# The last batch of a Mamba and mixture-of-experts layer: scans in two halves of 256 tokens, and experts without sorting

## The reference, cut to what matters

```python
x, z = split(in_proj(h))                      # 1024 inner channels each
x = silu(causal_conv4(x) + conv_b)
dt_lo, B, C = split(x_proj(x))                # 32, 16, 16
delta = softplus(dt_proj(dt_lo) + dt_b)
state[n] = exp(delta * A[n]) * state[n] + delta * x * B[n]   # over 512 tokens, for 16 states n
y = sum_n(C[n] * state[n]) + D * x
h = layernorm(h + out_proj(y * silu(z)))
logits = h @ gate.T                           # 8 experts, the best 2, softmax over the 2
h = layernorm(h + sum_over_2(w * (expert[e] @ h + expert_b[e])))
```

## Time and profile before

| what | value |
| --- | --- |
| median of 3 executions | 2401.52 us (2400.4 to 2407.32) |
| the profiled execution's own time | 2402.95 us |
| its span, first to last instruction | 2401.1 us |
| mean granted TensorE clock | 0.907 of full |
| busy: TensorE, VectorE, ScalarE, GpSimd | 87%, 87%, 63%, 76% |
| last scan ends at | 2221.6 us |

### The profile page before, as it was taken

One profiled execution on the slowest core, in us unless ns is written; L12 is line 12 of the kernel. 1 busy time (PEld: TensorE's weight loads), 2 busy tenths in 40 slices (PEclk: granted clock), 3 DMA queues, 4 the chain that ended last, 5 costly groups with the idle time before them and its releaser, 6 DMA issues.

```text
span 2401.1 us, 29781 instructions
## 1 busy us (share of the span) xinstructions
PE 2088.5 (87%) x8544; PEld 1217.3 (51%) x8544; DVE 2080.6 (87%) x2284; ACT 1516.3 (63%) x2586; POOL 1817.9 (76%) x1460
## 2 busy tenths in 40 slices
PE   7886879898989989899889989899898989888874
PEld 2444555555545555545545555545555555554532
DVE  3799999999999899998999989989999889999400
ACT  3747755785577766677577765768566775545322
POOL 1859997788887888779887888869887788776212
PEclk9897789898998999999899999989998899779887
DMA  3412031357544574356743674436752475477394
GB/s 99 145 53 84 19 125 60 114 176 256 155 111 145 198 263 123 106 165 216 269 110 116 210 265 130 128 137 207 257 133 91 156 244 180 127 233 235 76 378 120
DMA packets 210752, 385.08 MB, mean 160 GB/s; under 512 B 29048, under 2 KB 29304, under 8 KB 210592
## 3 DMA queue, kind: packets, MB, share of 16 engines
q1 hardware_dynamic: 196256, 349.63, 43.5%
q0 software_dynamic: 14336, 33.56, 6.7%
HBM read 297.15 MB, written 85.98 MB: 160 GB/s over the span
## 4 chain that ended last, share of the span: by engine, by line
DVE 27%; PE 22%; POOL 18%; issue 11%; ACT 4%; DMA 3%; SPq 1%; DVEq 0%; POOLq 0%; ACTq 0%
DVE hst L1432 14%; PE bank L873 13%; POOL dbu L1268 11%; DVE y L1290 7%; PE hTp L885 5%; DVE u L1318 2%; POOL u L1256 2%; POOL delta L1253 2%; PE bank L991 1%; DMA zs<-sorted_tokens 1%; ACT tokT L1143 1%; ACT dA L1180 1%; PE hTp L919 1%; DVE st L1296 1%; POOL sorted_tokens L1204 1%
## 5 line engine op out<-in xcount | busy, mean ns | idle before, releaser
L1268 POOL TENSOR_TENSOR dbu<-u,Bbc 128x512 f32<-128x512 f32 x1024 | 1308.1, 1313 | 298.0 <-DVE hst L1432 293.1
L1432 DVE TENSOR_TENSOR_SCAN hst<-dA,dbu 128x512 f32<-128x512 f32 x1024 | 1200.4, 1205 | 29.1 <-ACT dA L1180 25.9
L1180 ACT ACTIVATE dA<-delta,negA 128x512 f32<-128x512 f32 x1024 | 701.9, 689 | 477.8 <-DVE hst L1432 475.9
L885 PE MATMUL hTp<-ident,hst 128*128 128x128 f32 x4096 | 592.1, 298 | 124.5 <-DVE y L1290 43.9
L885 PEld LDWEIGHTS hTp<-ident,hst 128*128 128x128 f32 x4096 | 515.8, 154 | 363.9 <-DVE y L1290 143.9
L1290 DVE SCALAR_TENSOR_TENSOR y<-hTp,Ct,y 128x1024 f32<-128x1024 f32 x512 | 646.0, 1262 | 41.8 <-PE hTp L885 38.4
L873 PE MATMUL bank<-wslot,hidT 128*128 128x512 f32 x512 | 241.7, 607 | 16.7 <-ACT zs L1132 13.0
L873 PE MATMUL bank<-delta,tokT 128*128 128x512 f32 x536 | 248.3, 600 | 4.1 <-issue 2.2
L873 PE MATMUL bank<-wslot,tokT 128*128 128x512 f32 x496 | 236.5, 607 | 6.6 <-ACT tokT L1143 4.7
L873 PE MATMUL bank<-hidT,wslot 128*128 128x512 f32 x384 | 190.2, 639 | 12.8 <-DVE u L1318 9.7
L1318 DVE SCALAR_TENSOR_TENSOR u<-bank,cw,u 128x511 f32<-128x511 f32 (+2 forms) x192 | 142.3, 743 | 32.9 <-ACT u L1065 28.0
(11 more groups left out here) (131 smaller groups left out, 2238.8 us busy)
## 6 DMA issues: line engine op xcount, KB each, us to landing
wslot<-in_w_expT SPq DMA_DIRECT2D x86, 1024.0 KB
Bbc<-b_scratch SPq DMA_DIRECT2D x128, 256.0 KB
sorted_results<-ysb SPq DMA_DIRECT2D x113, 256.0 KB, 5.8
zs<-sorted_tokens SPq DMA_DIRECT2D x105, 256.0 KB, 4.0
wslot<-in_w_inT SPq DMA_DIRECT2D x26, 1024.0 KB
res<-in_w_expT SPq DMA_DIRECT2D x18, 1024.0 KB, 5.7
gate_scratch<-zs SPq DMA_DIRECT2D x64, 256.0 KB, 2.0
spare<-gate_scratch SPq DMA_DIRECT2D x56, 256.0 KB, 5.2
```

The lines of the kernel that those rows point to most:

```text
L885: mm = nc.tensor.transpose(hTp[i % 2][:, tok(j)], hst[n % 2][:, j, tok(i)], ident[:, :])
L1180: nc.scalar.activation(dA[j % 2][:, :], delta[w.odd][:, j, :], ACT.Exp, scale=negA[:, j, n:n + 1]).then_inc(exp_done, 1)
L1268: nc.gpsimd.tensor_tensor(dbu[j % 4][:, :], u[w.odd][:, j, :], Bbc[n % 2][:, :], ALU.mult).then_inc(dbu_done, 1)
L1432: nc.vector.tensor_tensor_scan(hst[n % 2][:, j, :], dA[j % 2][:, :], dbu[j % 4][:, :], 0.0, ALU.mult, ALU.add).then_inc(scan_done, 1)
```

## The change

Four things change.

1. `SEG_EPI` scans batch 7 in two halves of 256 tokens, all 16 states of the first half and then all of the second: 256 steps of half the length. ScalarE's and VectorE's instructions become 256 of 256 tokens; GpSimd's stay 128, each for two channel tiles; the transposition groups and additions stay 64 of 128 tokens, two a state and half, one for every four steps. The last column of each first-half scan is kept in `hst` and is the start of the second-half scan. B is loaded in 32 half rows.
2. Under the second half stand the first half's multiplication by z, output projection, normalization and gating, and its first six experts (`gyF` to `denF`). The experts are not sorted: each of the two tiles is multiplied by each expert (four matrix products) and VectorE adds the product with the token's weight, zero for experts not chosen, to `res` (`den`, `denF`). Experts 0 to 5 are loaded one after the other (`load_F`); 3 to 7 stay for the tail.
3. `SEG_LAST` has the same for tiles 2 and 3: `yT`, `out`, `ln1`, `x1T`, `logits`, gating for two tiles, then 20 dense products (experts 6 and 7 for tiles 0 and 1, all 8 for tiles 2 and 3), bias, normalization and store. Count, place, scale, scatter, the sorted tiles of batch 7 and `SEG_END` are gone. Experts 0 to 2 are loaded again (`load_D`). The gate values of batch 6 are loaded in four loads of 512 KB to places of their own (`szE`) in place of eight of 256 KB through two buffers. The bonuses of `SEG_EPI` and its pace are others.
4. In the segments from batch 3 on, ScalarE's eviction of the previous segment's last sorted tile (the eleventh) stands after the exponential of the second step, not before that of the first. This holds at five boundaries.

The planner's orders of `SEG_TWO` and `SEG_FULL` are otherwise the same. The diff, cut to its core:

```diff
+FIRST_EXPERTS = 6
+KEPT_SLOTS = [15, 16, 0, 1, 14, 15, 16, 0]
+GONE = range(NE - 5)
+KEPT = range(NE - 5, NE)
+LAST_DEN = [(t, e) for t in range(PAIR) for e in range(FIRST_EXPERTS, NE)] + [(t, e) for t in range(PAIR, NT) for e in [*KEPT, *GONE]]
...
+        "load_F": [("sp", 0.5, [(("gy", 4 * k + 3), "pool", 0.1)] if k < 2 else [(("moe", TILES - 5 + k), "pe", 0.1)] if k < 5 else [(("denF", 2 * (k - 5) + 1), "pe", 0.1)])],
+        "gyF": [("pool", 1.4, [(("row", 132 + 4 * (k // HALF)), "dve", 0.1), (("next_z", NT - 1), "sp", 4)])],
+        "yTF": [("pe", turn, [(("gyF", k), "pool", 0.1), (("outF", k // HALF - 1), "pe", 0), (("moeL", TILES - 1), "pe", 0)]), ("act", 0.6, [(x, "pe", 0.1)])],
+        "outF": [("pe", mm, [(("yTF", 2 * k + 1), "act", 0.1)]), ("dve", 1.8, [(x, "pe", 0.1), (("next_res", k), "sp", 6)])],
+        "lnF": [("act", 1.7, [(("outF", k), "dve", 0.1)])],
+        "x1TF": [("pe", turn, [(("lnF", k), "act", 0.1)]), ("act", 0.6, [(x, "pe", 0.1)])],
+        "logF": [("pe", 1.2, [(("x1TF", k), "act", 0.1)])],
+        "gateF": [("dve", 1.8, [(("logF", 1), "pe", 0.1)]), ("act", 0.3, [(x, "dve", 0.1)])],
+        "routeF": [("dve", 1.2, [(("gateF", 0), "act", 0.1)])],
+        "wTF": [("pe", 0.7, [(("routeF", 0), "dve", 0.1)]), ("act", 0.6, [(x, "pe", 0.1)])],
+        "denF": [("pe", mm, [(("x1TF", k % PAIR), "act", 0.1), (("logF", 1), "pe", 0), (("load_F", k // PAIR), "sp", 8)] if name == "denF" else []),
+                 ("dve", 0.75, [(x, "pe", 0.1), (("routeF", 0), "dve", 0)] + [(("denF", k - 2), "dve", 0)] * (k > 1))],
...
+def part_rows(halved):
+
+    return [2 * r for r in range(NH + 1)] + list(range(3 * NH, 2 * STEPS, NH)) if halved else list(range(0, STEPS, 2))
...
+SEG_EPI = Segment(by_urgency({"L0": 1114, "L1": 620, "mw": 161, "m0": 117, "ld": 51, "oe": -588, "of": 483, "ln": -83, "sc": 157, "mb": -398, "m1": -167, "E0": -758, "E1": 716, "m2": 204, "m3": 279, "m4": -375, "nz": -189, "ha": 293, "hd": 241, "lz": 54}), 0.45,
+                  W_EPI + W_O + GAP + [experts(2, TILES) + KEPT_IN[14], KEPT_IN[15], KEPT_IN[16]], [], 2 * STEPS)
+LAST_ROWS = [x for t in range(PAIR, NT) for x in [("yT", HALF * t + h) for h in range(HALF)] + [("out", t), ("ln1", t), ("x1T", t), ("logits", t)]]
+SEG_LAST = Segment([("load_D", e) for e in GONE] + LAST_ROWS + [("gate", 1), ("route", 1), ("wT", 1)]
+                   + [x for i in range(len(LAST_DEN)) for x in [("den", i)] + [("bias", t) for t in range(NT) if ("den", i) in last_den(t)]]
+                   + [x for t in range(NT) for x in (("fest", t), ("fln2", t), ("fstore", t))] + END, 0, W_LAST, [], 0)
...
+        def early_z(t, first, stop):
+
+            if t < PAIR:
+                return hT[:, HALF * t + first:HALF * t + stop, :]
+            return u[0][:, HALF * t + first:HALF * t + stop, :]
...
+        def part_of(q, halved):
+
+            per = PAIR if halved else NH
+            n, c, i = q // per % NS, q // per // NS, q % per
+            return n, PAIR * c + i, columns(n, c, halved)[0] + i * P
+
+        def columns(n, c, halved):
+
+            if not halved:
+                return 0, L
+            first = NS // 2 - n // 2 if c == 0 else 0
+            return first, first + HL
+
+        def decay_of(step, halved):
+
+            if halved:
+                return dA[step // 2 % 2][:, step % 2 * HL:(step % 2 + 1) * HL]
+            return dA[step % 2][:, :]
...
+                elif name == "load_F":
+                    e = x[1]
+                    if e < 2:
+                        sync.wait_ge(gy_done, w.e * (HALF * NT) + PAIR * HALF * (e + 1))
+                    else:
+                        s, v = w.bank(("moe", TILES - 5 + e) if e < 5 else ("denF", 2 * (e - 5) + 1))
+                        sync.wait_ge(bank_full[s], v)
+                    sync.sem_inc(seen_sp, 1)
+                    sync.dma_start(slot_of(w, KEPT_SLOTS[e]), block_src(("We", e))).then_inc(w_loaded[KEPT_SLOTS[e]], 16)
...
-                            sync.wait_ge(dbu_done, w.b * (NS * ND) + n * ND)
+                        if not (w.seg is SEG_PRO and m == 0):
+                            sync.wait_ge(dbu_done, w.b * (NS * ND) + m * (ND // 2 if w.seg.halved else ND))
                             sync.sem_inc(seen_sp, 1)
-                        if n + 1 < NS:
-                            load_B(w.b, n + 1)
...
-                    pe.wait_ge(acc_done, G * NH + (i - 1))
+            def state_part(b, q, halved, first, turns):
+
+                n, _, start = part_of(q, halved)
+                per = PAIR if halved else NH
+                if q % per == 0:
+                    pe.wait_ge(scan_done, b * (NS * ND) + (q // per + 1) * ND)
+                if not (first and q < 2):
+                    pe.wait_ge(acc_done, b * (NS * NH) + (q - 1))
                 if not (isinstance(turns, int) and turns == 0):
                     pe.wait_ge(turned_taken, turns)
                 for j in range(ND):
-                    mm = nc.tensor.transpose(hTp[i % 2][:, tok(j)], hst[n % 2][:, j, tok(i)], ident[:, :])
+                    mm = nc.tensor.transpose(hTp[q % 2][:, tok(j)], hst[n % 2][:, j, start:start + P], ident[:, :])
...
+                elif name in ("den", "denF"):
+                    t = LAST_DEN[x[1]][0] if name == "den" else x[1] % PAIR
+                    final = w if w.tail else w.final
+                    if share == 0:
+                        pe.wait_ge(turned_taken, (w.before.final if name == "den" and t < PAIR else final).turn(("x1T", t))[2])
+                    mm = accumulate(ps[:, :], lambda i: x1_turned(final, t)[:, tok(i)], lambda i: W[:, i, :], KD, share)
...
+            def decay(w, step):
+                n, j, halved = step // ND % NS, step % ND, w.seg.halved
+                cols = slice(step // STEPS * HL, (step // STEPS + 1) * HL) if halved else slice(0, L)
+                scans = max(step - 2, -1) if halved else step - 1
+                if step < ND:
                     act.wait_ge(u_ready, w.b * ND + (j + 1))
-                if not (w.seg is SEG_PRO and n == 0 and j < 2):
-                    act.wait_ge(scan_done, w.b * (NS * ND) + (n * ND + j - 1))
-                nc.scalar.activation(dA[j % 2][:, :], delta[w.odd][:, j, :], ACT.Exp, scale=negA[:, j, n:n + 1]).then_inc(exp_done, 1)
+                if not (w.seg is SEG_PRO and step < 2) and not (halved and step % 2):
+                    act.wait_ge(scan_done, w.b * (NS * ND) + scans)
+                nc.scalar.activation(decay_of(step, halved), delta[w.odd][:, j, cols], ACT.Exp, scale=negA[:, j, n:n + 1]).then_inc(exp_done, 1)
...
+                    if step == 1 and w.b > 2 and w.seg.steps:
+                        piece(w.before, ("moe", LATE - 1))
                     for x in pieces:
-                        piece(w, x)
-
-            periods(act, period, period, period)
+                        if w.seg is not SEG_FULL or x != ("moe", LATE - 1):
+                            piece(w, x)
+
...
+                    elif w.seg.halved and j % 2 == 0:
+                        k, cols = step // 2, slice(n // NS * HL, (n // NS + 1) * HL)
+                        if j == 0:
+                            pool.wait_ge(b_loaded[n % 2], w.b * (16 * NS // 2) + 16 * (n // 2 + 1))
+                        if n == 0:
+                            pool.wait_ge(u_ready, w.b * ND + (j + 2))
+                        pool.wait_ge(scan_done, w.b * (NS * ND) + (k - 3 if k < 4 else 2 * k - 6))
+                        nc.gpsimd.tensor_tensor(dbu[k % 4][:, :].rearrange("p (k t) -> p k t", k=2), u[w.odd][:, j:j + 2, cols],
+                                                Bbc[n % 2][:, cols].unsqueeze(1).broadcast_to((P, 2, HL)), ALU.mult).then_inc(dbu_done, 1)
...
+                elif name in ("den", "denF"):
+                    t, e = LAST_DEN[x[1]] if name == "den" else (x[1] % PAIR, x[1] // PAIR)
+                    dve.wait_ge(wt_ready, NB + t // PAIR)
+                    before = [i for i in range(x[1]) if LAST_DEN[i][0] == t] if name == "den" else []
+                    if before:
+                        sl, vl = w.bank(("den", before[-1]))
+                        dve.wait_ge(bank_taken[sl], vl)
+                    elif name == "den" and t < PAIR:
+                        sl, vl = w.before.bank(("denF", PAIR * (FIRST_EXPERTS - 1) + t))
+                        dve.wait_ge(bank_taken[sl], vl)
+                    elif name == "denF" and e > 0:
+                        sl, vl = w.bank(("denF", x[1] - PAIR))
+                        dve.wait_ge(bank_taken[sl], vl)
+                    nc.vector.scalar_tensor_tensor(res[:, t, :], ps[:, :], wt[:, t, e:e + 1], res[:, t, :], ALU.mult, ALU.add).then_inc(bank_taken[s], 1)
...
+                    elif w.seg.halved:
+                        c = n // NS
+                        start, stop = columns(n % NS, c, True)
+                        kept = columns(n % NS, 0, True)[1] - 1
```

(35 more changed lines are left out.)

466 lines of the change are left out of this document (280 added, 186 removed).

## The result

The changed kernel took a median of **2393.95 us** (20 executions, 2388.04 to 2401.65) beside 2407.02 for the kernel before in the same sessions (20 executions, 2394.7 to 2421.09). The ratio is 0.9952, with a 95% interval of 0.9938 to 0.9967: 13.1 us faster on the medians, where 2350 us, some 51 us faster, was forecast, and outside the range of 2328 to 2382. So the spans differ by less than the medians do, and I compare stretches rather than spans.

What follows compares the result with a forecast made beforehand. VectorE was taken to set the last batch's pace, with TensorE having room, before a serial tail of 180 us. 2402.95 + 37 (scans) - 78.5 (tail) - 10 (boundaries) = 2351.5, against the median 2350 us; range 2328 to 2382.

Steps and rivals of the forecast that it cites:

- The last batch's scans: Last batch, 256 half-length scans with first-half work added: 37 us longer, to 287 us (range +22 to +60).
- the tap: Second-half scans starting from a memory column: 0.055 us more each, 7 us for 128, from a similar instruction (0.743 against 0.69).
- The tail: From the last scan to the program's end: 101 us instead of 179.5, so -78.5 us (range -66 to -86).
- 33.5: After the last scan: about 26 us to the output's end, then 6.7 us to the last logit, summed as 33.5.
- That is the balance of a steady batch (258 and 253.5 in 277.2): Last batch's scans: VectorE 267 us and TensorE 249 at full clock balance like a steady batch, giving 287 us.
- the first rival: Second half of the last batch's scans: TensorE binds, 156 us of work in about 143, +24 to 2374 us; chance 0.20.
- the 11: Second half of the last batch: about 11 us more because kept experts 2 to 4 load only after tiles 12 to 14.
- The boundaries: Five batch boundaries: moving the eviction removes a 2.99 us VectorE wait, 2.5 us gained each, taken as -10 us (range 0 to 14).
- TensorE idles 3 us right after, so nothing is late: Behind each batch boundary: TensorE's 3 us of idle time means the earlier start, 2.5 us gained, makes nothing late.
- The late B rows: Last batch: SyncE's B half rows come late for GpSimd; at 2 us late per load, 2415 us; chance 0.05.
- a sign of being wrong: Last batch: GpSimd waiting for B was listed among the observations that would show the forecast wrong.
- Cheaper scans: Last batch: scans cost nothing more and VectorE keeps 95%, +22 to +25, tail -85, boundaries -12: 2330 us; chance 0.12.

Runs made afterwards that it cites:

- runs with four experts: Changed kernel with four instead of six first-half experts under the scans, the other four of tiles 0 and 1 behind the last scan: 2397.27 us, 0.9959.
- four products left out: Changed kernel without experts 4 and 5 of tiles 0 and 1 (four dense products and their additions, result incomplete): 2371.6 us, 0.9878.
- the other plan: Changed kernel without the eviction's move and with other priorities in the last segment's plan: 2385.03 us, 0.9925.

## Why the prediction was wrong

The direction and most parts of the working held; the size failed in two terms.

**1. The last batch's scans: forecast 287 us, measured 283.2.** Right. The forecast of 0.60 us for a scan's own time holds: two first-half scans take 1.18 us to the next addition's start (1989.94 to 1991.12), 0.59 each, and four later ones 2.33 (2136.85 to 2139.18), 0.58 each. Four second-half scans take 2.58 (2262.82 to 2265.40), 0.645 each. The start from a column in memory costs 0.059 by the means of the groups (731 against 672 ns), where 0.055 was taken from the tap. All 256 cost 128 x 0.59 + 128 x 0.645 - 128 x 1.12 = 14.7 us more than before; 17 were forecast. Of the 14.7, 128 x 0.055 = 7 are the start column, which leaves 7.7 for twice as many instructions.

**2. The tail: forecast 101 us, measured 126.2.** From the transposition of the last states on it is 102.3, as forecast (one step of that sum, 33.5, should read 26 + 6.7 = 32.7; its 2 us for stretches at the lower clock were an estimate, and the granted clock there was 0.98). What stands before it are 23.9 us of dense products for the first half. **The step that failed** is this one: "That is the balance of a steady batch (258 and 253.5 in 277.2)". TensorE's work was counted rightly: I had 269 us in the segment, and the 242.3 that it holds with the 23.9 that were left over are 266.2. But I compared two sums over the whole segment, while the added work has a place in time. The segment still had 40.9 us of TensorE's time idle; 31.2 of them lie in the first half, before any output of the first 256 tokens can exist and while the sorting of batch 6 holds up its experts. The second half had 9.7 us left, fewer than three products, and VectorE only 2.8. So it went as the first rival said, and its sum fits: it had 156 us of TensorE's work behind the middle, and 131.9 + 23.9 = 155.8 were measured. That is 14 more than the 141.6 of time there, where it had 13; the 9.7 of idle time make up the rest of the 23.9, where it had 11. That the 11 came out so near is partly luck: it stood for the loading of the kept experts, and behind the middle TensorE waits for no expert's weights, but for scans (3.4 us), for ScalarE's copies (3.2), for sorted rows (1.7) and for VectorE's additions (1.3). Even the middle was early: the scans of the first 256 tokens ended 12 us behind it. The places came at 107.9 us into the segment (before 111). The four separate loads of gate values, which I had counted against the rival, and the new order together brought them only 3 us forward. The granted clock was higher where TensorE was denser, as I had also held against it (0.97 with TensorE 93% busy in the second half, 0.81 with 78% in the first), though not in every stretch (0.50 from 2078 to 2086 us, with TensorE busy all the time); the work still did not fit. The runs with four experts, with four products left out and with the other plan show that TensorE's work from the middle on is conserved. I gave this case a chance of 0.20, with its arithmetic on the page: 156 us into 143. It should have been the forecast.

**3. The boundaries: forecast -10 us, measured +8.6 and +9.3 (+4.6 on the kernel before).** Here the sign was wrong. The step was: "TensorE idles 3 us right after, so nothing is late". I looked 4 us ahead. The local gain is there (3.91 us between the additions in place of 6.50), but some 20 us later a read of sorted rows, issued behind 2 MB of others, arrives when it always did. TensorE, moved forward, waits 4 us for it. The reordered read takes this wait away, and with it the move costs nothing. But it brings nothing either, so the wait explains the loss of about 9 us and not the missing gain of 10. The gain is given back a second time half a batch later, where VectorE waits longer for the C projection, as the table shows. The forecast had taken 2.5 us off for stretches led by TensorE or by loads; they took all of it. What makes that projection late with the move stays open.

**The sum.** The last batch: forecast -41.5, measured -17.5 to -20 by the three profiles and -19 to -20 by the ratios of the kernels without the move. In the first profile the difference is +23.9 for products left over, -3.6 for scans and +1.3 for the rest of the tail. The boundaries: -10 forecast, about +9 measured. Together -11, against a measured -13.1 with an interval of 8 to 15.

**The other rivals.** The late B rows did not come: GpSimd waited for B once in the segment (6.8 us; in the second and third trace twice, 17 to 18 us in all), which was a sign of being wrong, but VectorE lost at most 2.5 us to GpSimd's product in any of the three. "Cheaper scans" was not the case, though the scans did come out a little cheaper than forecast. ScalarE's exponentials, costed at nothing, cost nothing: ScalarE was busy 160.9 of the 283.2 us, and no wait for dA is in the list of VectorE's waits there, whose smallest is 0.3 us.

**What is best.** Two complete kernels beat both: the changed one without the move (2384.9 and 2385.0; with the sorted rows first 2384.7, with the other plan 2385.0) and the one with the move and the sorted rows read first (2384.0). No run tells them apart. Against the kernel before each is about 22 us faster, 0.8 to 1%.

## What to carry to other kernels

Before work is put under a stage with idle time, split that stage at the moment when the new work can first start, and compare busy time with elapsed time behind that moment for every engine; the idle time ahead of it is worth nothing to that work (here 31.2 of TensorE's 40.9 us). Where a stall is removed, look through the whole period behind it, and first at the transfers that its work waits for, not just at the next instructions: with the move alone, the scans began 2.8 us earlier and the read behind other reads in the queue was issued at 875.41 us instead of 875.67. Moving that read forward with the work that it feeds brought the waits for it down from 19.0 us over the changed kernel to 2.5.

## What the hardware showed that I had not expected

With a start from a column in memory a scan of 256 elements takes 59 ns longer than from a constant (731 against 672 ns, 128 instructions each). It is not the state of the stretch: from 2127 to 2160 us, where both kinds stand, the means are 729 and 669 ns.

A 256 KB read of sorted rows takes 3.2 us from issue to landing as the median of the program, but 10.1 from 862 to 898 us, where the reads ahead of it in the queue keep the DMA engines full (a share of 0.92 over this stretch, 1.05 from 880 to 895). Issuing it ahead of them, at the same total of bytes, was worth 10 us over the program with the move, and nothing without it. The 0.9 MB taken out of that queue at each boundary was worth about 16 us with the move and 3 without: the price of the same bytes depended on whether a 3 us wait stood at the boundary.
